# A state space scan with units of 64 steps and carries summed on GpSimd

## The reference, cut to what matters

```python
def _L1_attn_ref(x, W_in, W_delta, W_B, W_C, W_out, A, D):
    xs, z = jnp.split(x @ W_in, 2, axis=-1)
    delta = xs @ W_delta
    Bv, Cv = xs @ W_B, xs @ W_C
    deltaA = jnp.exp(jnp.einsum('bld,dn->bldn', delta, A))
    deltaB = jnp.einsum('bld,bln->bldn', delta, Bv)
    def step(state, inp):                  # state: (batch, d=128, n=128)
        dA_i, dB_i, x_i, C_i = inp
        state = dA_i * state + dB_i * x_i[:, None, :]
        return state, jnp.einsum('bdn,bn->bd', state, C_i)
    ...                                    # 1024 steps
    return (y * jax.nn.silu(z)) @ W_out
```

## Time and profile before

| what | us |
| --- | --- |
| median of 3 runs (lowest, highest) | 6915.71 (6912.54, 6920.44) |
| the profiled execution, its own time | 6921.82 |
| its span | 6920.0 |
| DVE busy in the span | 6286.0 |
| of it the full scans, L1057 | 4465.4 |
| POOL: token DMA issues, L989 | 1090.0 |

### The profile page before, as it was taken

The page is one execution under the profiler, slowest core; times in us unless marked ns, Lnnn a source line. Parts: engine busy times, 40 slices in busy tenths (PEclk is TensorE's granted clock), DMA queues, the critical chain, the costliest instruction groups (busy, mean ns, idle before and its releaser), DMA issues. The chain is left out here.

```text
span 6920.0 us, 147961 instructions
## 1 busy us (share of the span) xinstructions
PE 6346.8 (92%) x52737; PEld 4042.9 (58%) x52737; DVE 6286.0 (91%) x3976; ACT 4605.5 (67%) x9719; POOL 2423.6 (35%) x3276
## 2 busy tenths in 40 slices
PE   8999989999879999999999999999999999998867
PEld 4666735566546566565665666656666566665535
DVE  7888878888769999999999999999999999999962
ACT  7888868888546666666666666666666666666541
POOL 5555545555433233333333323333233332332200
PEclk9999999999979999999999999999999999999985
DMA  6666666666522122121121211212122121221164
GB/s 143 154 154 154 154 146 155 155 154 154 135 58 63 43 49 53 39 63 45 47 53 40 63 45 47 52 41 64 43 47 53 46 58 43 48 51 39 24 188 114
DMA packets 864186, 566.76 MB, mean 82 GB/s; under 512 B 594957, under 2 KB 768941, under 8 KB 863661
## 3 DMA queue, kind: packets, MB, share of 16 engines
q1 hardware_dynamic: 794045, 526.01, 32.0%
q0 software_dynamic: 69632, 34.22, 2.2%
HBM read 161.99 MB, written 125.17 MB: 41 GB/s over the span
## 5 line engine op out<-in xcount | busy, mean ns | idle before, releaser
L1057 DVE TENSOR_TENSOR_SCAN states<-decay,enter_ps 128x1024 f32<-128x1024 f32 x2048 | 4465.4, 2262 | 77.3 <-ACT enter_ps L905 74.5
L764 PEld LDWEIGHTS enter_ps<-s_steps,s_tokens 128*128 128x128 bf16 (+1 forms) x16384 | 1598.3, 129 | 1450.0 <-DVE states L1057 1217.2
L764 PE MATMUL enter_ps<-s_steps,s_tokens 128*128 128x128 bf16 (+1 forms) x16384 | 2116.4, 309 | 313.9 <-DVE states L1057 306.9
L890 ACT ACTIVATE decay<-rate_ps 128x504 f32<-128x504 f32 x4096 | 2196.5, 588 | 186.2 <-PE rate_ps L741 7.2
L741 PE MATMUL rate_ps<-s_wide,s_decays 128*128 128x256 bf16 x8192 | 1322.6, 283 | 15.4 <-ACT decay L890 7.7
L243 POOL TENSOR_TENSOR entered<-gates 128x512 f32<-128x512 f32 x512 | 900.4, 1759 | 889.0 <-ACT gates L203 889.0
L905 ACT COPY enter_ps<-states 128x16 f32<-128x16 f32 x1920 | 362.9, 189 | 1270.1 <-PE enter_ps L764 1267.4
L989 POOL DMA_DIRECT2D s_tokens<-tokens_dram x2176 | 1090.0, 509 | 153.5 <-PE enter_ps L764 115.2
L788 PE MATMUL y_ps<-states,spread 128*32 128x512 f32 x8320 | 1113.1, 607 | 0.8 <-ACT y_sb L913 0.8
L161 PE MATMUL pre<-rows,weights_left 128*32 128x512 f32 x8192 | 908.9, 596 | 36.3 <-POOL rows L236 23.8
L741 PEld LDWEIGHTS rate_ps<-s_wide,s_decays 128*128 128x128 bf16 x8192 | 890.7, 118 | 80.3 <-ACT decay L890 20.3
(11 more groups left out here) (145 smaller groups left out, 2456.5 us busy)
## 6 DMA issues: line engine op xcount, KB each, us to landing
rows<-feat SPq DMA_DIRECT2D x1024, 132.0 KB, 2.4
rows<-feat SPq DMA_DIRECT2D x512, 128.0 KB, 2.4
s_steps<-steps_dram SPq DMA_DIRECT2D x4096, 8.0 KB
rows<-feat SPq DMA_DIRECT2D x512, 127.8 KB, 2.4
s_wide<-rates_dram SPq DMA_DIRECT2D x1024, 32.0 KB, 1.9
s_tokens<-tokens_dram POOLq DMA_DIRECT2D x2048, 16.0 KB, 2.0
rates_dram<-parts SPq DMA_DIRECT2D x64, 384.0 KB, 3.3
steps_dram<-parts SPq DMA_DIRECT2D x64, 384.0 KB, 3.5
```

The lines of the kernel that those rows point to most:

```text
L764: mm = pe.matmul(out.rearrange("p h l -> p l h"), tokens[s][0:n * TERMS, k, :], steps[s][0:n * TERMS, k, 0:n, d:d + half], start=True, sto ...
L890: act.activation(decay[i][:, HEADS // 2 * h:HEADS // 2 * (h + 1), 1:], rate_ps[h][:, :, 0:n], ACT.Exp).then_inc(decay_ready, 1)
L1057: dve.tensor_tensor_scan(out, factor, term, 0.0, ALU.mult, ALU.add).then_inc(scanned, 1)
```

## The change

Full chunks now hold 64 steps, without a carry column, so that 16 chunks cover the 1024 steps and the short chunk is gone (128 units a batch, two buffer sets). The carry is added to the first step's enter value: PE computes the first step of all 128 d of the next chunk by a matmul into work_ps in unit 5 (`first_steps`), ACT copies it to SBUF in unit 7 (`take_first_steps`), and POOL for every unit multiplies column 0 of the decay by the last state of the chunk before, sets that column to zero, and adds the product to the first step (`carry` in the GpSimd block). ACT's carry copy then takes this sum in place of the last state; in chunk 0 there is none. Exponents are made three units ahead in place of two, decays two in place of one. The inverse fill moves from unit 5 to unit 4, the reciprocal from before unit 4 to before unit 3, the drain of that stage from unit 6 to 5. POOL's stage pieces are placed in slots of units. The token loads move from POOL to SP, into `load` behind the steps. The gate has two pieces of 4 x 128.

```diff
 SPAN = 64
-FULL = SPAN - 1
-CROWD = LEN // FULL
-LAST = LEN - CROWD * FULL
-CPB = CROWD + 1
+CPB = LEN // SPAN
...
-        SETS = 3
+        SETS = 2
...
+        product = [sb(f"product{i}", [STATE, HEADS]) for i in range(2)]
+        at_first = [sb(f"at_first{s}", [STATE, INNER]) for s in range(SETS)]
...
             def load(b, c):
...
-                sp.wait_ge(rate_ready, halves_to(b, before(c) + 1))
+                sp.wait_ge(rate_ready, halves_to(b, c - 1))
...
-                sp.wait_ge(enter_ready, units_to(b, before(c) + 1))
+                sp.wait_ge(enter_ready, units_to(b, c - 1))
...
+                for e in range(TERMS):
+                    a = STATE * (e // SPLITS)
+                    src = tokens_dram[bass.ds(b, 1), t0:t0 + SPAN, a:a + STATE].rearrange("b (k t) n -> (b t) k n", t=BLOCK)
+                    sp.dma_start(tokens[s][e::TERMS, :, :], src).then_inc(tokens_in[s], DMA)
...
+            def first_steps(b, c):
+                s = set_of(c)
+                pe.wait_ge(enter_in[s], SCAN0 + (turn_of(b, c) + 1) * BLOCK * DMA)
+                pe.wait_ge(tokens_in[s], SCAN0 + (turn_of(b, c) + 1) * TERMS * DMA)
+                pe.wait_ge(drained, stages_to(b + 1, c) if b + 1 < BATCH else stages_to(b + 1, 0))
+                pe.wait_ge(at_first_ready, firsts_to(b, c))
+                pe.matmul(work_ps[:, 0:INNER], tokens[s][:, 0, :], steps[s][:, 0, 0, :], start=True, stop=True
+                          ).then_inc(first_filled, 1)
...
             def unit(b, u, first, ending):
...
-                if not ending or u + 2 < UPB:
-                    exponents(*following(b, u + 2))
...
+                if not ending or u + 3 < UPB:
+                    exponents(*following(b, u + 3))
+                if c:
                     contract(b, c - 1, g)
                 elif not first:
...
+                    contract(b - 1, CPB - 1, g)
+                if g == 1 and not ending:
                     fill(b + 1, c)
-                if g == 5 and c < len(STAGES) and not ending:
+                if g == 4 and not ending:
                     fill_inverse(b + 1, c)
+                if g == 5 and c + 1 < CPB:
+                    first_steps(b, c + 1)
...
             def carry(b, c, g, i):
-                act.wait_ge(enter_ready, units_to(b, c) + g + 1)
                 if c:
...
+                    act.wait_ge(enter_ready, units_to(b, c) + g + 1)
+                    act.wait_ge(added, carries_to(b, c) + g + 1)
+                    act.wait_ge(decay_reset, carries_to(b, c) + g + 1)
+                    act.copy(enter_ps[i][:, :, 0], at_first[set_of(c)][:, HEADS * g:HEADS * g + HEADS]).then_inc(carried, 1)
+
+            def take_first_steps(b, c):
+                act.wait_ge(first_filled, firsts_to(b, c) + 1)
...
+                act.copy(at_first[set_of(c)][:, :], work_ps[:, 0:INNER]).then_inc(at_first_ready, 1)
...
                 carry(b, c, g, u % 2)
-                if not ending or u + 1 < UPB:
-                    decays_of(*following(b, u + 1))
-                if c < len(STAGES) and not ending:
+                if not ending or u + 2 < UPB:
+                    decays_of(*following(b, u + 2))
+                if g == 7 and c + 1 < CPB:
+                    take_first_steps(b, c + 1)
...
-            def load_tokens(b, c):
...
+            def carry(b, c, g):
+                if c:
+                    n, i, mine = carries_to(b, c) + g, g % 2, slice(HEADS * g, HEADS * g + HEADS)
+                    pool.wait_ge(decay_ready, halves_to(b, c) + 2 * g + 2)
+                    pool.wait_ge(scanned, units_to(b, c - 1) + g + 1)
+                    pool.wait_ge(added, n - 1)
+                    pool.sem_inc(passed, 1)
+                    pool.tensor_tensor(product[i][:, :], decay[g % RING][:, :, 0], states[set_of(c - 1)][:, mine, SPAN - 1],
+                                       ALU.mult).then_inc(product_ready, 1)
+                    pool.wait_ge(product_ready, n + 1)
+                    pool.memset(decay[g % RING][:, :, 0], 0.0).then_inc(decay_reset, 1)
+                    pool.wait_ge(at_first_ready, firsts_to(b, c) + 1)
+                    pool.tensor_tensor(at_first[set_of(c)][:, mine], at_first[set_of(c)][:, mine], product[i][:, :], ALU.add
+                                       ).then_inc(added, 1)
+
             def batch(b, ending):
...
+                for u in range(UPB):
+                    c, g = u // GROUPS, u % GROUPS
+                    carry(b, c, g)
+                    if g == 5:
+                        spread_out(b, c)
+                    if not ending:
+                        if g == 0 and c:
+                            differences(b + 1, c - 1, LATE)
+                        differences(b + 1, c, g)
...
-                    dve.wait_ge(carried, units_to(b, c) + g + 1)
+                    if c:
+                        dve.wait_ge(carried, carries_to(b, c) + g + 1)
+                    else:
+                        dve.wait_ge(enter_ready, units_to(b, c) + g + 1)
...
-    PIECES = ((0, 4, TOKENS), (4, 4, TOKENS), (8, 1, LAST))
+    PIECES = ((0, 4, TOKENS), (4, 4, TOKENS))
```

More of the change, by code:

```diff
@@ L409, in build_scan @@
         sem = Semaphores(nc, ctx, "scan")
-        SETS = 3
[L411 to L421, removed]
+        SETS = 2
+        NQ = SPAN // QUAD
+        room = [sb(f"states{s}", [STATE, INNER * SPAN + SPAN]) for s in range(SETS)]
+        states = [room[s][:, 0:INNER * SPAN].rearrange("p (d l) -> p d l", l=SPAN) for s in range(SETS)]
+        spread = [sb(f"spread{s}", [STATE, (NQ + 1) * REACH]) for s in range(SETS)]
+        readout = [sb(f"s_readout{s}", [STATE, SPAN]) for s in range(SETS)]
+        steps = [sb(f"s_steps{s}", [128, BLOCKS, BLOCK, INNER], BF16) for s in range(SETS)]
+        tokens = [sb(f"s_tokens{s}", [128, BLOCKS, STATE], BF16) for s in range(SETS)]
+        wide = [sb(f"s_wide{s}", [128, GROUPS, QUAD, SPAN], BF16) for s in range(SETS)]
         decay = [sb(f"decay{i}", [STATE, HEADS, SPAN]) for i in range(RING)]
-        decay_end = [sb(f"decay_end{i}", [STATE, HEADS, LAST + 1]) for i in range(RING)]
+        product = [sb(f"product{i}", [STATE, HEADS]) for i in range(2)]
+        at_first = [sb(f"at_first{s}", [STATE, INNER]) for s in range(SETS)]
         y_sb = [sb(f"y_sb{i}", [128, QUAD, INNER]) for i in range(2)]
-        none = sb("none", [STATE, HEADS])
         ident = sb("s_ident", [128, 128])
@@ L771, in enters @@
-                mm.then_inc(enter_ready, 1)
+                for k in range(BLOCKS):
+                    for h in range(2):
+                        d, half = HEADS * g + HEADS // 2 * h, HEADS // 2
+                        out = enter_ps[i][:, half * h:half * h + half, BLOCK * k:BLOCK * k + BLOCK]
+                        mm = pe.matmul(out.rearrange("p h l -> p l h"), tokens[s][:, k, :],
+                                       steps[s][:, k, :, d:d + half], start=True, stop=True)
+                mm.then_inc(enter_ready, 1)
@@ L944, in _ @@
             pool.memset(steps[0][:, :, :, :], 0.0)
-            pool.memset(steps[2][:, :, :, :], 0.0)
-            pool.memset(none[:, :], 0.0)
             pool.memset(decays[:, :, :, :], 0.0)
             for s in range(SETS):
-                pool.memset(room[s][:, EDGE + INNER * span[s]:], 0.0)
+                pool.memset(room[s][:, INNER * SPAN:], 0.0)
                 z = pool.memset(spread[s][:, :], 0.0)
@@ L1014, in _ @@
             for n in range(len(STAGES)):
-                differences(0, n)
-            load_tokens(0, 0)
-            spread_out(0, 0)
+                for slot in range(LATE + 1):
+                    differences(0, n, slot)
             for b in range(BATCH):
@@ L1028, in _ @@
                 dve.memset(decay[i][:, :, :], 0.0)
-                dve.memset(decay_end[i][:, :, :], 0.0)
             for s in range(SETS):
@@ L1163, in turn_y @@
                         mm = pe.matmul(turned_ps[n][:, tokens * k:tokens * k + tokens], y[i][:, first + k, :],
-                                       (place if tokens == TOKENS else place_end)[:, :], start=True, stop=True)
+                                       place[:, :], start=True, stop=True)
                     mm.then_inc(turned, 1)
```

236 lines of the change are left out of this document (83 added, 153 removed).

## The result

| | us |
| --- | --- |
| before, median of 4 runs (lowest, highest) | 6917.34 (6912.54, 6920.44) |
| changed kernel, median of 4 runs | 6803.31 (6802.24, 6806.17) |
| ratio, 95% interval | 0.9836 [0.9819, 0.9853] |
| profiled execution after: its own time, span | 6804.26, 6802.5 |

The account below looks back on a forecast made before the run. DVE's scans were taken as the bound. From the profiled 6921.8, -118.8 - 7.1 + 7.5 + 3.4 - 2 gave 6804.8; that execution lay 6.1 above the median, so the forecast was 6799 us, range 6785 to 6845.

Parts of the forecast that it names:

- The bound: On DVE: full scans run without any gap at 2.178 us each, except in the eight short scans ending a batch.
- Short units gone: At the fifteen batch boundaries: removing the eight short units saves 118.8 us, 7.51 us at each of eleven boundaries.
- the fill's stall: Chunk 1, inverse fill moved to unit 4 on PE: one scan 0.5 us late, 15 times, adding 7.5 us.
- POOL's chain: Product, memset and sum per carry unit on POOL: 0.9 us with waits (0.4 to 3.5), hidden, adding 0 us.
- the near rows: Profile rows on POOL near a 128x16 sum in size: 128x16 memset 121 ns, 128x16 copy 215 ns.
- the far one: Profile row on POOL far above a 128x16 sum: a full 128x512 sum, 1156 ns.
- One matmul, one copy per chunk: PE's first-steps matmul in unit 5, 0.13 us, and ACT's copy in unit 7, about 0.2 us: both hidden.
- Tokens on SP: Eight token issues per chunk moved from POOL to SP's queue: 0.42 us each, 3.4 us per chunk, nothing slips.
- the ends: Range given for one token issue on SP: 0.34 to 0.98 us.
- the 4.4 us of cover: Time between a load's steps and tokens landing, by 3072.4, and the new matmul wanting them at 3076.8.
- Start: First enter products wait for tokens issued behind the steps: 3.4 us later, once.
- End and gate: After the last scan, 7.1 us in place of 14.2, saving 7.1; gate phase, 2 us saved.

Follow-up runs that it names:

- nocarry: Changed kernel with the whole carry left out (first-steps matmul and copy, POOL's three operations, ACT's carry copy): 6798.79 us.
- nosqrt: Changed kernel with a plain copy in place of the Sqrt of the norm's variance on ScalarE: 6795.68 us.
- allthree: inv5 plus the reciprocal again before unit 4 of chunk 1 and the very first chunk's token loads on ScalarE's queue: 6791.28 us.
- inv5: Changed kernel with the inverse fill back in unit 5 of chunk 1, its drain and that chunk's first-steps matmul in unit 6: 6796.56 us.

## Why the prediction was right, step by step

- **The bound** (DVE's scans, without a gap): right. 125 in a row at 2.178, nocarry the same. That the short units held the only gaps was not quite so: in chunk 1 the scans of units 3 and 4 were already 0.19 and 0.29 late before.
- **Short units gone, less the inverse fill**: 118.8 - 7.5 = 111.3 predicted. From the first scan's start to the end of the last full scan it is 4477.46 in place of 4587.71: 110.25. Per undisturbed batch 286.79 - 279.84 = 6.95 against 7.51 - 0.5 = 7.01. Of this the fill's stall is 0.53 for 0.5, at the scan named.
- **Missed, and without price**: the scan of unit 4 in chunk 1, late by 0.29, before as after. I had moved the reciprocal without asking what it covered: ACT behind its table loads (nosqrt, allthree). All that stood beside scans and short units was 286.79 - 278.78 - 7.51 = 0.50 us per batch before and is 279.84 - 278.78 = 1.06 now; 0.53 of the difference of 0.56 is the fill, and allthree, with the reciprocal back in its place, has the period of inv5; so its move changed nothing. The difference is 8.4 us in 15 batches where I had 7.5.
- **POOL's chain** at 0.9 us: it takes 0.59, the two-input operations 241 and 220 ns, at the near rows and not the far one. Hidden, as said. The threshold beside it was wrong: "costs nothing up to about 2 us" and "from 2.20 the gain is gone", while 1.58 already costs 22 us and 2.01 the whole gain. I divided idle time by units and asked for latency at a few places only.
- **One matmul, one copy per chunk**: recorded at 0.22 and 0.27 us, for 0.13 and 0.2. Hidden: from chunk 2 of the first batch on, only two scans outside the chunks 1 are late, by 0.14 us each.
- **Tokens on SP**: 0.63 us per issue, not 0.42, within the ends. Steps and tokens of one load are out at 3074.14, where I had 3071.1, and the last has landed at 3075.52; the new matmul runs at 3077.16, where I had 3076.8. So 1.6 of the 4.4 us of cover are left there. Elsewhere none is: in chunk 9 of three batches PE stands idle before that matmul. Below, the last of eight token loads landed at 2973.16. Hidden all the same, since PE caught up before a scan was due; for these the prediction was lucky.

```profile
2966.48 5.30 SPq L629 DMA_DIRECT2D s_tokens<-tokens_dram  x8
2973.25 0.22 PE L759 MATMUL stage_ps<-s_steps,s_tokens 128*128 128x128 bf16 x1 [0.46 <-issue]
```

- **Start**: first scan 1979.34 for 1976.50, +2.84, for +3.4. The first enter products come at 1977.35 against 1974.29.
- **End and gate**: last scan to last store 6.85 in place of 14.2, 7.35 less for 7.1; with what follows it, the gate above all, 10.1 less for 9.1.
- **Sum**: 2.84 - 110.25 - 10.1 = -117.5 on the span for -117.0. That it is this close is in part luck: one term was off by 1.05 us one way, two by 0.6 and 1.0 the other. The 4.3 us between 6799 and the median 6803.31 is none of the terms: I had carried over that the profiled execution of before lay 6.1 above the median, and that of after lies 1.0 above.

## What to carry to other kernels

Where one engine runs without a gap, count what it does besides its main work per batch, and put helper work on any engine with time, even a slower one; a tenth of a microsecond 1920 times on the bound engine outweighed 0.6 us as often beside it. Average idle time doesn't say what a helper engine can take: ask how long before its use the data is ready, and what can stand in the queue ahead of it, a block of DMA issues above all. When a small instruction is moved, ask what wait it had been hiding.

## What the runs showed of the hardware that was not expected

- A DMA issue on SP costs by the issue: 0.63 us for a token load, 0.68 for half of one, 0.34 for a step load.
- Token loads begun by POOL had an unexplained pause of 3.18 us in its issuing before issue 128 and every 120th after it, in two kernels, and none in the kernel before. On SP's queue two token issues of one load never start more than 1.85 us apart.
- In a stream of scans a 128x16 product on DVE is recorded as 192 ns and delays the stream by 0.09 to 0.10.
- A change of ACT's function and back put two loads of 1.28 us on it.
